# A four-layer fp32 network on one core: bonus and level 0 of the linear attention in one pass, narrow levels 4 and 5, layer 2's projection weights in layer 1's memory, first norm ahead of the constants

## The reference, cut to what matters

```python
xa = _ln(x, ln1_w, ln1_b)
sx = concatenate([state[:, 1:2] - xa[:, :1], xa[:, :-1] - xa[:, 1:]], axis=1)
xxx = tanh((xa + sx * maa_x) @ maa_w1).reshape(b, l, 5, DM)      # DM = 32
xxx = einsum('blfd,fde->blfe', xxx, maa_w2)
xm = xa[:, :, None] + sx[:, :, None] * (maa_stack + xxx)
xk, xw, xv, xr, xg = (xm[:, :, j] for j in range(5))
w = exp(-exp(time_decay + tanh(xw @ td_w1) @ td_w2))
r, k, v = xr @ Wr.T, xk @ Wk.T, xv @ Wv.T                        # 32 heads of 16
g = silu(xg @ Wg.T)
def step(s, rkvw):
    a = k_t[..., :, None] * v_t[..., None, :]
    out = einsum('bhi,bhij->bhj', r_t, u * a + s)
    s = a + w_t[..., :, None] * s
og = normalised out * gn_w + gn_b
x1 = x + og * g @ Wo.T
... # channel mix: xk2, xr2 of _ln(x1); x1 + sigmoid(xr2 @ Wfr.T) * (relu(xk2 @ Wfk.T)**2 @ Wfv.T)
```

## Time and profile before

| what | us |
|---|---|
| median of 3 runs | 2489.3 (2488.08 to 2489.41) |
| the profiled execution | 2494.95 |
| its span in the trace | 2492.6 |
| PE busy in the span | 2331.0 (94%) |
| DVE, ACT, POOL busy | 1111.1, 1082.6, 552.4 |
| end of layer 1's work, start of `layers23` | about 1203 |
| decay of the first, second, fourth and last batch (ACT L1830) | 1259.12, 1330.23, 1479.08, 2358.9 |

### The profile page before, as it was taken

One profiled execution on the slowest core, in us unless ns is written; L12 is line 12 of the kernel. 1 busy time (PEld: TensorE's weight loads), 2 busy tenths in 40 slices (PEclk: granted clock), 3 DMA queues, 4 the chain that ended last, 5 costly groups with the idle time before them and its releaser, 6 DMA issues. The chain is left out here.

```text
span 2492.6 us, 59022 instructions
## 1 busy us (share of the span) xinstructions
PE 2331.0 (94%) x22880; PEld 1720.1 (69%) x22880; DVE 1111.1 (45%) x3070; ACT 1082.6 (43%) x3409; POOL 552.4 (22%) x585
## 2 busy tenths in 40 slices
PE   7886999999999999999488999999999999999986
PEld 3444667777777666667276878777777877777864
DVE  5662222222222222222234565655666655665542
ACT  4552333333333333333112655555555455555544
POOL 0001010110000000000023334333333343343320
PEclk9997999999999999999678999999999999999998
DMA  5421000000000000000600000111000011100010
GB/s 165 168 89 65 15 18 18 22 18 18 18 18 18 18 18 18 18 10 5 191 15 16 21 17 14 25 25 25 20 20 12 23 25 25 25 20 16 10 25 14
DMA packets 117056, 81.93 MB, mean 33 GB/s; under 512 B 79136, under 2 KB 91680, under 8 KB 114720
## 3 DMA queue, kind: packets, MB, share of 16 engines
q1 hardware_dynamic: 107744, 54.32, 8.2%
q0 software_dynamic: 2240, 12.58, 1.5%
q10 hardware_dynamic: 6912, 12.59, 1.3%
HBM read 62.68 MB, written 12.58 MB: 30 GB/s over the span
## 5 line engine op out<-in xcount | busy, mean ns | idle before, releaser
L745 PEld LDWEIGHTS bank<-normedT,mlp_w 128*128 128x128 f32 x2048 | 235.7, 193 | 18.3 <-issue 17.1
L745 PE MATMUL bank<-normedT,mlp_w 128*128 128x128 f32 x2048 | 241.7, 278 | 0.8 <-DVE normedT L975 0.8
L755 PE MATMUL bank<-mlp_w,geluT 128*128 128x512 f32 x512 | 228.9, 595 | 0.0
L1638 PEld LDWEIGHTS quad<-rT,k_even_odd 32*128 32x128 f32 x6144 | 187.2, 193 | 39.5 <-DVE wkv_scores L2095 29.7
L926 DVE CUSTOM_DVE_ANT_0 probs<-quad,neg_mask 128x256 f32<-128x256 f32 x256 | 90.8, 421 | 273.8 <-PE quad L675 273.8
L1638 PE MATMUL quad<-rT,k_even_odd 32*128 32x32 f32 x6144 | 197.9, 278 | 13.9 <-DVE wkv_scores L2095 11.5
L2095 DVE COPY_PREDICATED wkv_scores<-level_masks,quad 128x1024 f32<-128x1024 int32 x96 | 160.6, 1673 | 93.4 <-PE quad L1638 93.4
L1930 ACT ACTIVATE scores<-scores,nmax 128x128 f32<-128x128 f32 x512 | 198.9, 400 | 2.9 <-DVE nmax L2185 2.9
L933 DVE COPY probsT<-quad 128x512 f32<-128x512 f32 x128 | 84.9, 683 | 191.9 <-PE quad L689 191.7
L755 PEld LDWEIGHTS bank<-mlp_w,geluT 128*128 128x128 f32 x512 | 93.6, 190 | 103.4 <-issue 103.4
L1445 POOL TENSOR_TENSOR k_even_odd<-k_even_odd,decay_products 128x512 f32<-128x512 f32 x80 | 95.9, 1199 | 275.9 <-PE quad L1638 275.9
(11 more groups left out here) (238 smaller groups left out, 4463.7 us busy)
## 6 DMA issues: line engine op xcount, KB each, us to landing
x_in<-in_x SPq DMA_DIRECT2D x32, 256.0 KB, 3.0
mlp_w<-in_mlp_w POOLq DMA_DIRECT2D x8, 1024.0 KB, 5.5
ctx_in<-in_ctx SPq DMA_DIRECT2D x16, 256.0 KB, 2.9
l_out<-wy ACTq DMA_DIRECT2D x16, 256.0 KB, 2.2
wy_in<-l_out SPq DMA_DIRECT2D x16, 256.0 KB, 3.4
hT<-in_ctxT SPq DMA_DIRECT2D x16, 256.0 KB, 3.5
l_out<-l_x ACTq DMA_DIRECT2D x16, 256.0 KB, 2.0
x_in<-l_out SPq DMA_DIRECT2D x16, 256.0 KB, 3.0
```

What stands on the lines that cost most here:

```text
L745: mm = nc.tensor.matmul(PS[b][:, f * P:(f + 1) * P], mlp_w1[:, c, m * P:(m + 1) * P], nT[:, c, :], start=(c == 0), stop=(c == NC - 1))
L755: mm = nc.tensor.matmul(PS[M.bank][:, :], gT[:, f, :], mlp_w2[:, f, :], start=(f == 0), stop=(f == NF - 1))
L1638: mm = nc.tensor.matmul(PS[r][:, at:at + SB], keys(rr, c, s), odd, start=True, stop=True)
```

## The change

1. Bonus and level 0 become one pass. ACT writes the keys into two tensors: `K2` gets the odd tokens, a new `K0` the even ones; POOL's `p_k0` puts the odd keys times u into `K0`; `p_ur` makes `rm`, r times u on even tokens and r alone on odd ones. Level 0 multiplies `K0` with `rm` over all 64 tokens, and one predicated copy of 2048 elements with a new mask writes both kinds of score. `p_diag` goes. Level 0's decay products (`p_rup` 0, `p_kup` 0) no longer wait for level 0.
2. Levels 4 and 5 load only the keys that are wanted: level 4 has 64 matmuls of 32 loaded and 16 streamed columns for 32 of 128 and 32, level 5 has 32 of 64 and 32. Level 5's merge is a plain copy on 64 partitions.
3. `p_t5` has tokens on its rows, 4 matmuls of 160 streamed columns; ACT's tanh writes the fifth factor four times, two transposes (`p_t5t`) and a copy bring it back, and `p_mix4` uses four row groups and the four banks of `quad`.
4. The gate: ACT writes tanh alone, DVE takes the other factor from PSUM.
5. Memory: Wk, Wr, Wv and the raw Wg lie in q_w's, k_w's, v_w's and out_w's memory and are loaded at the end of layer 1. Wo3 follows in raw Wg's place. The output shares the fourth score tile. Wo, Wfk, Wfr, Wfv, Wq3, Wk3 and Wv3 are issued by ACT at the block's start, behind no wait.
6. The first turn, which holds only n of batch 0, comes ahead of the constants and memsets (`after_first`); POOL orders Wg instead of DVE.
7. `ORDER` and `USES` are new on all engines.

The diff, cut to its core:

```diff
@@ -551,6 +552,11 @@
                     sp.wait_ge(s_negm, i)
                     sp.wait_ge(A.free, A.read(i - 1, 6))
                     load_ctx(i)
+
+                O = ring("o")
+                sp.wait_ge(O.free, O.read(B - 1, 2))
+                for t, n in zip((q_w, k_w, v_w, out_w), ("Wk", "Wr", "Wv", "Wg")):
+                    sp.dma_start(t[:, :, :], a[n]).then_inc(s_w2, 16)
...
+        W = {n: sb(n, [P, NC, D]) for n in ("Wg", "Wo", "Wfk", "Wfr", "Wfv", "Wq3")}
+        W["Wk"], W["Wr"], W["Wv"], wgraw = shared
+        W["Wo3"] = wgraw
...
@@ -1282,6 +1290,8 @@
 
             for i in range(last):
                 step(*(i - k if i >= k else None for k in range(last + 1)))
+                if i == 0:
+                    segments["after_first"]()
             for k, b in banks.items():
                 b.enter_loop([r for bank, r in USES.values() if bank == k])
...
                 load_x(0)
-                for n in ("Wk", "Wr", "Wv"):
-                    sp.dma_start(W[n][:, :, :], a[n]).then_inc(s_w2, 16)
-                for c in range(NC):
-                    sp.dma_start(wgraw[c], a["Wg"][:, c, :]).then_inc(s_wgraw, 16)
...
-                for h in range(HC):
-                    sp.dma_start(W["Wo"][D2 * h:D2 * (h + 1), :, :], a["Wo"][h:P:HC, :, :]).then_inc(s_w3, 16)
-                for n in ("Wfk", "Wfr", "Wfv"):
-                    sp.dma_start(W[n][:, :, :], a[n]).then_inc(s_w3, 16)
-                for t, n in ((W["Wq3"], "Wq3"), (Wk3, "Wk3"), (Wv3, "Wv3"), (W["Wo3"], "Wo3")):
-                    sp.dma_start(t[:, :, :], a[n]).then_inc(s_w4, 16)
-                steps(sp, "sp", dict(n_lds0=n_lds0, n_ldx=n_ldx, p_ldw=p_ldw, w_lda=w_lda, p_v=p_v))
+
+                def after_first():
+
+                    sp.wait_ge(s_wg, NC)
+                    sp.dma_start(W["Wo3"][:, :, :], a["Wo3"]).then_inc(s_w4, 16)
+
+                steps(sp, "sp", dict(after_first=after_first, n_lds0=n_lds0, n_ldx=n_ldx, p_ldw=p_ldw, w_lda=w_lda, p_v=p_v))
...
+                def after_first():
+
+                    for t in (AD[:, :, :], V2[:, :, :], u1[:, :], v3[:, :, :, :]):
+                        nc.gpsimd.memset(t, 0.0).then_inc(s_zero, 1)
+                    for c in range(NC):
+                        nc.gpsimd.tensor_copy(W["Wg"][:, c, :].rearrange("p (m h j) -> p m h j", m=NC, j=D2),
+                                              wgraw[:, c, :].rearrange("p (m j h) -> p m h j", m=NC, j=D2)).then_inc(s_wg, 1)
...
+                    nc.gpsimd.tensor_tensor(rm[:, :, :].rearrange("p c (n two) -> p c n two", two=2),
+                                            rT[:, :, :].rearrange("p c (n two) -> p c n two", two=2),
+                                            ue[:, :, :].unsqueeze(2).to_broadcast([P, NC, HALF, 2]), ALU.mult).then_inc(s_ur, 1)
+
+                def p_k0(i, uses):
+
+                    u = uses[("p_k",)]
+                    pool.wait_ge(u.free, u.done)
+                    odd = [t[:, :, :, :].rearrange("p c (n two) e -> p c n (two e)", two=2)[:, :, :, 2:4] for t in (K0, K2)]
+                    nc.gpsimd.tensor_tensor(odd[0], odd[1], CS("u").unsqueeze(2).unsqueeze(3).to_broadcast([P, NC, HALF, 2]), ALU.mult)\
+                        .then_inc(s_k0, 1)
...
+                    if lv:
+                        u = uses[("p_level", lv)]
+                        pool.wait_ge(u.ready, u.made)
+                    else:
+                        u = uses[("p_k",)]
+                        pool.wait_ge(u.free, u.done)
                         pool.wait_ge(s_wl, (LV - 1) * (i + 1))
...
-                        mm = nc.tensor.matmul(PS[b][0:DM, P:2 * P], maa_w1[:, c, P:P + DM], z[:, c, :],
-                                              start=(c == 0), stop=(c == NC - 1))
+                        mm = nc.tensor.matmul(PS[b][:, 0:NM * DM], z[:, c, :], maa_w1[:, c, :], start=(c == 0), stop=(c == NC - 1))
                     mm.then_inc(u.ready, 1)
 
+                def p_t5t(i, uses):
+
+                    u, b = uses[("p_t5t",)], BANK["p_t5t"]
+                    claim(u)
...
                     for m in range(NC):
-                        mm = nc.tensor.matmul(PS[b][:, m * P:(m + 1) * P], maa_w2b[0:DM, m * P:(m + 1) * P], t5b[:, :],
-                                              start=True, stop=True)
+                        r = slice(DM * m, DM * m + DM)
...
                 def p_u1(i, uses):
...
+                def keys(t, rr, c, s, n=HALF):
+
+                    return t[rr, c, s:s + n, :].rearrange("p s e -> p (s e)")
...
-                    if lv:
+                    if lv == 0:
+                        pe.wait_ge(s_k0, i + 1)
+                        pe.wait_ge(s_ur, i + 1)
...
+                                    if lv == 0:
+                                        mm = nc.tensor.matmul(PS[r][:, at:at + HALF], keys(K0, rr, c, s), rm[rr, c, s:s + HALF],
+                                                              start=True, stop=True)
+                                    else:
+                                        odd = rT[rr, c, s:s + HALF].rearrange("p (n two w) -> p n two w", two=2, w=n)[:, :, 1, :]
+                                        mm = nc.tensor.matmul(PS[r][:, at:at + SB], keys(K2, rr, c, s), odd, start=True, stop=True)
+                            elif lv < 6:
+                                for b in range(SB // n):
+                                    for r in range(RG):
+                                        rr, s = slice(SB * r, SB * r + SB), HALF * bh + 2 * n * b
+                                        mm = nc.tensor.matmul(PS[r][4 * n * b:4 * n * b + 2 * n, at + n * b:at + n * b + n],
+                                                              keys(K2, rr, c, s, n), rT[rr, c, s + n:s + 2 * n], start=True, stop=True)
+                        if lv == 6:
...
                     token_major(uses[("b_out",)], BANK["b_out"], W["Wo3"], rows(attnT))
 
-                steps(pe, "pe", dict(n_xa=n_xa, p_t5=p_t5, p_mix=p_mix, p_mix4=p_mix4, p_u1=p_u1, p_w=p_w, p_k=p_k, p_r=p_r, p_v=p_v,
-                                     p_g=p_g, p_diag=p_diag, p_level=p_level, p_s0=p_s0, p_av=p_av, p_av6=p_av6, w_var=w_var,
+                steps(pe, "pe", dict(after_first=after_first, n_xa=n_xa, p_t5=p_t5, p_t5t=p_t5t, p_mix=p_mix, p_mix4=p_mix4, p_u1=p_u1, p_w=p_w, p_k=p_k, p_r=p_r, p_v=p_v,
+                                     p_g=p_g, p_level=p_level, p_s0=p_s0, p_av=p_av, p_av6=p_av6, w_var=w_var,
                                      w_rstd=w_rstd, w_out=w_out, w_xc=w_xc, w_fk=w_fk, w_fr=w_fr, w_fv=w_fv, a_x=a_x, a_q=a_q,
                                      a_kv=a_kv, a_score=a_score, a_turn=a_turn, a_value=a_value, a_norm=a_norm, b_out=b_out))
...
+                def after_first():
+                    made_constant(nc.vector.tensor_scalar(bq[:, :], CS("bq3"), D3 ** -0.5, None, ALU.mult))
...
+                    made_constant(nc.vector.tensor_copy(ue[:, :, 0], CS("u")))
+                    assert n_setup == SETUP
+                    dve.wait_ge(s_setup, n_setup)
+                    dve.wait_ge(s_zero, 4)
+                    dve.wait_ge(s_w2, 16 * 4)
+                    for c in range(NC):
+                        nc.vector.tensor_reduce(wvm[:, c, :, :], W["Wv"][:, c, :].rearrange("p (m j h) -> p m h j", m=NC, j=D2), AX.X, ALU.add)\
+                            .then_inc(s_wvm, 1)
+                    dve.wait_ge(s_wvm, NC)
+                    nc.vector.tensor_scalar(wvm, wvm, 1.0 / D2, None, ALU.mult).then_inc(s_wvm, 1)
+                    dve.wait_ge(s_wvm, NC + 1)
+                    for c in range(NC):
+                        wv = W["Wv"][:, c, :].rearrange("p (m j h) -> p m j h", m=NC, j=D2)
+                        nc.vector.tensor_tensor(wv, wv, wvm[:, c, :, :].unsqueeze(2).to_broadcast([P, NC, D2, HC]), ALU.subtract)\
+                            .then_inc(s_wv, 1)
 
...
+                        dve.wait_ge(t.free, t.done)
+                    elif later(i):
+                        dve.wait_ge(s_ogc, i)
...
+                    n, at, m = 1 << lv, LAT[min(lv, 4)], HALF // 2 >> lv
+                    if lv == 0:
+                        op = nc.vector.copy_predicated(AD[:, :, :], lm[:, NLM:NLM + HALF].unsqueeze(1).to_broadcast([P, RG * NC * 2, HALF]),
+                                                       grid)
+                    elif lv < 5:
...
+                    else:
+                        op = nc.vector.tensor_copy(AD[0:HALF, :, SB:HALF], grid[0:HALF, :, 0:SB])
+                    op.then_inc(u.free, 1)
...
                             dve.wait_ge(s_attnT, i)
+                    if k == 3 and later(i):
+                        dve.wait_ge(s_store, 16 * i + 16)
```

294 lines of the change are left out of this document (136 added, 158 removed).

## The result

The changed kernel takes **2397.3 us** (median of four runs, 2397.03 to 2397.58) against 2489.36 (2488.08 to 2490.52) for the kernel before: ratio 0.963, with a 95% interval of 0.9614 to 0.9647. That is 92.1 us less; the prediction was 2398.4, 90.9 us less, with a range of 2378 to 2432. The profiled execution took 2397.57 us. So the total is met within 1.1 us, but partly by luck: the front gave 3 to 5 us less than put and the fifteen turns after the first 6 to 8 us more, by which of two profiles of the kernel before one compares with.

What follows compares the result with a forecast made beforehand. PE was taken to bound the steady turn, busy 73.03 of 73.35 us. Gains of 18.3 (block start), 7.5 (first turn) and 65.1 us (15 turns) sum to 90.9, giving 2398.4 us, range 2378 to 2432.

Steps and rivals of the forecast that it cites:

- the front: Start of layers 2 and 3, up to the first Wk matmul: gain 18.3 us, bounds 14 to 20.
- first turn, to the first product with the values: Low-clock chain of levels: bonus phase gone and level 5 loading half the columns, together 7.5 us less.
- the 15 turns after it: PE work only: 4.34 us less in each, a turn of 69.0 us, 65.1 us in all.
- tail: Turns after the last p step, with w, a and b only: work kept, nothing gained, give or take 2 us.
- Level 5: 64 loaded columns instead of 128, at 14.3 ns a matmul: 0.92 us, saves 1.0 a turn.
- Level 4: 128 matmuls for 64, loading 32 columns and streaming 16, at 14.3 ns: 1.83 us, saves 0.08 a turn.
- A: Levels 4 and 5: narrow matmuls cost by the instruction, 29.8 ns each; hence 2446 us; chance 0.09.
- B: A hand-over to PE becomes late, costing about 1 us in each of 16 turns: 2414 us; chance 0.15.
- Margin 1: ACT must drain p_mix4 from the score banks before a_score 0 starts; 1.6 us to spare.
- C: Block start: first x lands 15.8 us after issue beside ACT's loads, gain 5.8 us, 2411 us; chance 0.06.
- D: Score banks: ACT drains p_mix4 too late, making the kernel slower than before, about 2516 us; chance 0.01.
- E: Whole kernel: the change is neutral or does not do what it says; chance 0.01.

Runs made afterwards that it cites:

- wide4: Changed kernel with level 4 back in its old form, 64 matmuls that load 128 columns and stream 32: 2404.1 us.
- wide5: Changed kernel with level 5 back in its old form, 64 matmuls that load 128 columns instead of 64: 2412.3 us.
- mix4_one_group: Changed kernel with all eight matmuls of the fifth mixture in the first group of 32 rows, for time alone: 2407.4 us.
- x_alone: Changed kernel with one more wait: ScalarE issues its 14 weight loads only when x of batch 0 has landed: 2393.5 us.
- quiet_pool: Changed kernel with GpSimd's four clearings before x lands and its ordering of Wg held until z is ready: 2396.1 us.
- weights_late: Changed kernel with the four projection weights loaded behind x of batch 0 at the start of layers 2 and 3, not in layer 1: 2407.9 us.

## Why the prediction was right, and where it was not

The sum by its own terms, against the first profile of before and, in brackets, against the second:

| term | predicted | measured |
|---|---|---|
| layers 0 and 1 | 0 | 4.2 (0) |
| front, from the issue of x to the first Wk | 18.3 | 14.9 (13.4) |
| first turn, to the first product with the values | 7.5 | 6.9 (7.2) |
| the 15 turns after it | 65.1 | 71.2 (73.5) |
| tail | 0 ± 2 | 0.0 (−1.3) |
| sum | 90.9 | 97.2 (92.8) |

The offset of the profiled execution (5.6 us above the median) was taken off as a constant. The second profile, whose span is 4.4 us shorter, shows where it lay: 4.2 us ahead of the block and 1.5 in the front, and the rest of the program took 1.3 us less in the first.

**What bounds the kernel** was right. wide4, wide5 and mix4_one_group put back 0.57, 0.83 and 0.65 us of PE's work, and the steady turn grew by 0.57, 0.87 and 0.65.

**The steady turn** was predicted as 69.0 us and is 68.82; its saving of 4.34 is 4.53. Bonus phase 1.94 as put. t5: 0.5 put, 0.48 found, by two errors that cancel (the products 1.19 for 1.45, the two transposes 0.41 for 0.26). p_mix4: 0.85 put, from a duration of 1.15; from start to start it was 1.09 and is 0.43, which saves 0.66. Level 5: 14.3 ns put, 17.0 found, saves 0.83 for 1.0. Level 4: 14.3 put, 10.5 found, saves 0.57 for 0.08. (That is 4.48, less 0.04 for the new form of level 0; the last 0.09 I did not place.) The step that failed is the last two: I took one price, that of the product with the values, for two forms. The rows now give four prices for four row groups at once: 30.0 ns at 128 loaded columns, 17.0 at 64, 10.5 at 32, 8.7 at 16. The first three lie on 4 ns plus 0.2 ns a column, without a term for the streamed columns (32, 32, 16). The row with 32 loaded columns and 64 streamed, 14.3 ns, was too dear for level 4. Most likely its streaming bound it, but that is argued: it also differs in shape, 128 rows into four groups of columns, and no run varied the streamed columns alone. The Trainium skill has the fitting rule on the page "TensorE: Matmul & The Clock Gate", section "LDWEIGHTS (loading the stationary operand)": the time of a weight load goes by its columns, at 1.2 columns a ns, whatever the rows. Spread over four groups that is an estimate of 0.21 ns a column, and the slope of these rows, 0.2, agrees with it. The rule of the Trainium skill that the prediction cited, from "TensorEngine Tiling (Array Packing)", "Instruction Overhead", gave an estimate of 25 ns for both levels, and 10.5 and 17.0 do not bear that out. Within one group the four prices are 35 ns and more (four times 8.7), so whether a group by itself has such a floor no run here shows.

**The other turns.** The prediction took all 15 as steady. The second is not. There the chain of levels still waits and the clock is low for part of the time, and it shrank by 9.0 us (9.8 against the second profile) for 72.45, the largest single miss in the table: 4.7 us. The first row of each pair is the wait ahead of a level, the second a projection, before and after:

```profile
1350.00 1.99 PE L1638 MATMUL quad<-rT,k_even_odd 32*128 32x32 f32 x64 [1.27 <-DVE rT L2085]
1351.91 5.47 PE L1512 MATMUL bank<-ffn_k_in,Wfk 128*128 128x128 f32 x32
```

```profile
1318.10 1.99 PE L1665 MATMUL quad<-rT,k_even_odd 32*128 32x32 f32 x64
1320.02 3.84 PE L1537 MATMUL bank<-ffn_k_in,Wfk 128*128 128x128 f32 x32
```

The wait of 1.27 us is gone, and with it the 1.6 us that Wfk took longer at the low clock. What else makes up the 4.7 was not taken apart: another wait is 1.87 us where it was 1.70, and a wait of 4.70 for POOL's gn_squares has given way to one of 4.34 ahead of p_mix4, for ACT's xm. In the 14 other turns the gain is 62.1 us for 60.8 predicted: 14 times the 0.19 by which the steady turn saves more than put, less 1.2 for the odd turn's wait.

**The front** is where two steps failed and two smaller errors offset a part. Statistics: put 3.3 us after the issue of x, found 5.5. I had bounded the cost of ACT's loads beside it by nothing and 4 us and took 0.8; x_alone shows 2.9. From there to z ready: put 7.2, found 10.8, because GpSimd's clearings and its ordering of Wg moved beside these very instructions. I had said that POOL "has until the Wg projection and nothing else in that time" and asked only whether POOL would be late, not what it does to DVE. Constants: put 3.6, found 1.9, since the first of them, 1.70 us where it opened the block, took 0.16 here. The centring was 6.7 for 6.8, and the last leg 3.2 for 3.6. That sums to 3.5 us late, 28.0 for 24.55. The weights were there in time, though the row that the prediction read for it is of four quarters of Wg, 256 KB each: the four of 1 MB took up to 13.1 us from issue, 22 us ahead of the block. The Trainium skill has the mechanism on the page "SBUF — State Buffer", section "Who interferes with whom": VectorE and GpSimd share one pair of ports, whoever issues first holds it for a whole instruction, and copies, casts and tensor_scalar are among the operations that can want it, while reductions do not; an operation with two inputs in SBUF can be held up by GpSimd's reads. The rows of quiet_pool and weights_late agree as to which operations grow beside what: ln_x beside clearings, casts beside copies, shifted and z beside copies alone, reductions never. The 3.41 us of ln_x end 0.3 us behind the last of four clearings in a row (1206.63 to 1209.72), so here the pair did not change hands between the clearings. Who came first is not to be read here: the recorded start of ln_x, 1206.59, lies 0.04 us ahead of the first clearing's. With that page read against the moved memsets, the danger would have been seen ahead.

**Rivals.** A (price by instruction) fell: both levels got cheaper. B (a late hand-over) fell: in a steady turn PE idles 0.33 us before b_out, for 0.32 before. Margin 1, put at 1.6 us, is 2.5: ACT ends its copies of p_mix4 at 1972.1 and a_score 0 starts at 1974.56. C (x late) was partly true: x came 2.2 us later than put, for its 12.5. D and E fell with B: no hand-over to the score banks is late, and the change does what it says. What none of them named is the wait for instructions.

## What to carry to other kernels

An instruction that is moved to an idle engine must be asked twice: is that engine free, and does what it does there slow the neighbour on which the path runs? Price a narrow matmul by the columns it loads and those it streams, each from a row of its own, and stop splitting before the density of instructions brings waits with no releaser: 256 rows of narrow matmuls in one level cost 0.3 us a turn by themselves and some 3.6 by what followed. When you test one such edit, ask what your wait covers: weights_late waited for four weights where its first reader needs one. And take a second profile of the kernel before when the one at hand lies above its median: here 4 us of difference stood where nothing had changed.

## What the runs showed of the hardware that I had not expected

- A tensor_scalar of 128x512 on VectorE took 3.41 us beside four GpSimd memsets in a row and 0.55 without; casts of 128x30 grew from 0.17 to 1.12 us beside a GpSimd copy, while reductions beside the same copy did not change.
- PE stalls with no releaser where narrow matmuls stand densest: 2.04 us inside a level of 256 rows, and the granted clock then stood at 0.50 until about 6 us later, so that Wfk, with 32 rows, took 6.44 us for 3.84. The stall and the clock together cost more than the level. All 28 such stalls looked at end 1.2 to 1.6 us after a 16 KB packet of the instruction queue has landed.
- Of four weights of 1 MB each, issued beside 5.5 MB on another queue, the last landed 26.4 us after its issue, and 13.1 at the end of layer 1, beside little else; a transfer of 256 KB alone took 2.6 us and beside the first of those loads 5.5.
- The same program keeps its times to 0.6 us in one set of runs and spreads over 5 us in another; the profiles put most of the difference into the stretches at low or changing clock (second turn 63.4 to 65.9 us in variants with equal work, tail 95.4 to 97.7), while a single steady turn is longer by 0.3 us at most.
